# Two class look-ups, one on each half of the TensorE rows, in a fused conditioning kernel

## The reference, cut to what matters

```
h = _ln(x, pw_g[pathway_ids], pw_b[pathway_ids])
h = _ln(h, cp_g[compartment_ids], cp_b[compartment_ids])
t = _ln(x, tm_g[time_steps], tm_b[time_steps])
s = _ln(x, ms_g[scale_type], ms_b[scale_type])
m, n, r = x + _mlp_ln(...)            # one vector per batch entry each
cat = concat([w0*h, w1*t, w2*m, w3*n, w4*r, w5*s])
out = x + _ln(silu(cat @ W1 + b1) @ W2 + b2, g, b)
```

## Time and profile before

| what | value |
|---|---|
| time, median of 3 runs | 1038.83 us (1038.68 to 1039.85) |
| the profiled execution's own time | 1037.92 us |
| its span in the profile | 1036.0 us |
| granted TensorE clock, mean | 0.982 |

### The profile page before, as it was taken

One profiled execution on the slowest core, in us unless ns is written; L12 is line 12 of the kernel. 1 busy time (PEld: TensorE's weight loads), 2 busy tenths in 40 slices (PEclk: granted clock), 3 DMA queues, 4 the chain that ended last, 5 costly groups with the idle time before them and its releaser, 6 DMA issues.

```text
span 1036.0 us, 13671 instructions
## 1 busy us (share of the span) xinstructions
PE 973.5 (94%) x4404; PEld 800.4 (77%) x4404; DVE 805.5 (78%) x1103; ACT 267.7 (26%) x330; POOL 527.3 (51%) x625
## 2 busy tenths in 40 slices
PE   0968799999999999999999999999999999999994
PEld 0755578888888888888888888888888888888883
DVE  4953686969788787978878787978879697978844
ACT  2431222313122222223132231323132232312220
POOL 5650353737555463746555473745555374654311
PEclk9969989999999999999999999999999999999998
DMA  8466254553446354453545455443635445343121
GB/s 303 143 202 226 72 178 97 157 148 118 147 100 203 81 181 123 152 145 84 187 91 188 98 172 141 137 130 91 209 75 181 119 154 150 105 159 91 51 61 40
DMA packets 52786, 142.19 MB, mean 137 GB/s; under 512 B 10233, under 2 KB 10505, under 8 KB 48673
## 3 DMA queue, kind: packets, MB, share of 16 engines
q0 software_dynamic: 23168, 66.60, 26.0%
q1 hardware_dynamic: 29600, 75.37, 20.8%
HBM read 125.04 MB, written 16.91 MB: 137 GB/s over the span
## 4 chain that ended last, share of the span: by engine, by line
PE 90%; DVE 4%; DMA 2%; POOL 1%; issue 1%; SPq 0%; DVEq 0%; ACT 0%; POOLq 0%; ACTq 0%
PE hid_ps L1143 22%; PE hid_ps L1145 22%; PE hid_ps L1144 22%; PE o_ps L1225 5%; PE o_ps L1223 5%; PE o_ps L1224 5%; PE made_ps L1123 3%; PE made_ps L1136 3%; PE hid_ps L1148 1%; DMA y_sb<-ms_g 1%; PE o_ps L1084 0%; DMA r_sb<-res_W 0%; DVE yst L777 0%; DVE xc L716 0%; POOL xrs L387 0%
## 5 line engine op out<-in xcount | busy, mean ns | idle before, releaser
L1143 PE MATMUL hid_ps<-cat_hi,w_hi 128*128 128x512 f32 x1024 | 404.6, 395 | 27.2 <-POOL w_lo L463 25.2
L1144 PE MATMUL hid_ps<-cat_lo,w_hi 128*128 128x512 f32 x1024 | 400.8, 391 | 0.0
L1145 PE MATMUL hid_ps<-cat_hi,w_lo 128*128 128x512 f32 x1024 | 400.7, 391 | 0.0
L1143 PEld LDWEIGHTS hid_ps<-cat_hi,w_hi 128*128 128x128 f32 x1024 | 193.7, 189 | 68.6 <-issue 26.0
L1145 PEld LDWEIGHTS hid_ps<-cat_hi,w_lo 128*128 128x128 f32 x1024 | 193.6, 189 | 40.9
L1144 PEld LDWEIGHTS hid_ps<-cat_lo,w_hi 128*128 128x128 f32 x1024 | 193.7, 189 | 39.2
L445 POOL DMA_INDIRECT pw_rows<-cp,class_now x64 | 131.0, 2046 | 59.7 <-DVE y_sb L768 48.9
L581 ACT ACTIVATE cat_hi<-v_ring 128x1024 fp32r<-128x1024 f32 x64 | 68.0, 1062 | 307.1 <-DVE v_ring L750 307.1
L438 POOL DMA_INDIRECT pw_rows<-pw,path_now x64 | 101.6, 1587 | 61.2 <-DVE y_sb L786 41.0
L385 POOL TENSOR_TENSOR fve<-fmv,eps_col 128x1 f32<-128x1 f32 x64 | 40.1, 626 | 155.9 <-DVE fmv L805 155.9
L459 POOL DMA_DIRECT2D r_sb<-x x60 | 57.8, 964 | 111.1 <-DVE r_sb L834 100.4
(11 more groups left out here) (124 smaller groups left out, 1204.5 us busy)
## 6 DMA issues: line engine op xcount, KB each, us to landing
x_sb<-x SPq DMA_DIRECT2D x16, 1024.0 KB, 6.1
xc<-xT SPq DMA_DIRECT2D x16, 1024.0 KB, 5.0
out<-r_sb SPq DMA_DIRECT2D x64, 256.0 KB, 2.0
r_sb<-x POOLq DMA_DIRECT2D x60, 256.0 KB, 4.8
stats_bc<-token_stats SPq DMA_DIRECT2D x30, 256.0 KB, 5.0
ids_sb<-ids SPq DMA_DIRECT2D x16, 256.0 KB, 7.2
keep<-int_W SPq DMA_DIRECT2D x12, 256.0 KB, 6.5
r_sb<-int_W SPq DMA_DIRECT2D x12, 256.0 KB, 7.4
```

The source lines that it names most:

```text
L1143: pe.matmul(acc, w1_hi[:, k, cols], hi, start=start, stop=False)
L1144: pe.matmul(acc, w1_hi[:, k, cols], lo, start=False, stop=False)
L1145: return pe.matmul(acc, w1_lo[:, k, cols], hi, start=False, stop=stop)
```

## The change

The rows of the two tables are placed anew. The classes take partitions 0 to 63 (high part at 0, low part at 16, high part again at 32), the scales 64 to 127 with the same offsets. Each of a fill's two matmuls takes only the 64 partitions of its own table. The partitions that want the high part of the deviation are now 0 to 31 and 64 to 95, those that want the low part 32 to 63 and 96 to 127, so the statistics are read back by four transfers to 32 partitions each in place of two to 64. The low part of the tables no longer begins at a multiple of 32, and it is made by DVE over all partitions with a column of 0 and -1 (`tables()`), no more by POOL; `class_rows` does the same for `class_bias`. The parameter tensor `small` gets two more columns.

```
-HI, LO, AGAIN, SCL = 0, 32, 64, 16
+HI, LO, AGAIN, SCL = 0, 16, 32, 64
...
-                for v in range(2):
-                    sp.dma_start(stats_bc[64 * v:64 * v + 64, :, :, :].rearrange("q p s t -> q (p s t)"),
-                                 stats_dram[v].rearrange("p m -> (p m)").partition_broadcast(64)
-                                 ).then_inc(stats_in[v], 16)
+                for q in range(4):
+                    sp.dma_start(stats_bc[32 * q:32 * q + 32, :, :, :].rearrange("q p s t -> q (p s t)"),
+                                 stats_dram[q % 2].rearrange("p m -> (p m)").partition_broadcast(32)
+                                 ).then_inc(stats_in[q % 2], 16)
...
-            pool.wait_ge(tab_hi_done, 1)
-            pool.tensor_tensor(class_tab[LO:LO + 32, :, :], tab_raw[LO:LO + 32, :, :],
-                               class_tab[LO:LO + 32, :, :].bitcast(f32), ALU.subtract).then_inc(tables_ready, 1)
-            pool.wait_ge(tables_ready, 1)
             x_rstd(0)
             spread_first()
...
+            def tables():
+
+                dve.wait_ge(tab_hi_done, 1)
+                dve.scalar_tensor_tensor(class_tab[:, :, :], class_tab[:, :, :].bitcast(f32), less_low[:, 0:1], tab_raw,
+                                         ALU.mult, ALU.add).then_inc(tables_ready, 1)
+
...
-                dve.tensor_tensor(class_bias[AGAIN:AGAIN + 32, :], o_ps[AGAIN:AGAIN + 32, 1, :],
-                                  class_bias[AGAIN:AGAIN + 32, :].bitcast(f32),
-                                  ALU.subtract).then_inc(class_bias_ready, 1)
+                dve.scalar_tensor_tensor(class_bias[:, :], class_bias[:, :].bitcast(f32), less_again[:, 0:1], o_ps[:, 1, :],
+                                         ALU.mult, ALU.add).then_inc(class_bias_ready, 1)
...
                 x_low(0, 0)
                 x_low(0, 1)
+                tables()
                 sum_blocks(0)
...
                 for i in range(2):
-                    ins = pe.matmul(made_ps[:, i, :], class_tab[:, i, j * P:(j + 1) * P], scaled[:, :],
+
+                    rows = slice(SCL * i, SCL * i + 64)
+                    ins = pe.matmul(made_ps[:, i, :], class_tab[rows, i, j * P:(j + 1) * P], scaled[rows, :],
                                     start=True, stop=True)
```

More of the change, by code:

```diff
@@ L129, in build @@
         b1_cols, ib1_cols = part("b1T"), part("ib1T")
+        less_again, less_low = part("less_again"), part("less_low")
         sT, shifts, fold = part("sT", BATCHES), part("shifts", 5), part("fold")
@@ L413, in spread_first @@
                 pool.wait_ge(first_stats_out, 16)
-                for v in range(2):
-                    pool.dma_start(stats_bc[64 * v:64 * v + 64, :, :, :].rearrange("q p s t -> q (p s t)"),
-                                   stats_dram[v].rearrange("p m -> (p m)").partition_broadcast(64)
+                for q in range(4):
+                    pool.dma_start(stats_bc[32 * q:32 * q + 32, :, :, :].rearrange("q p s t -> q (p s t)"),
+                                   stats_dram[q % 2].rearrange("p m -> (p m)").partition_broadcast(32)
                                    ).then_inc(first_stats_in, 16)
@@ L704, in stats_here @@
                 if isinstance(b, int) and b == 0:
-                    dve.wait_ge(first_stats_in, 32)
+                    dve.wait_ge(first_stats_in, 64)
                 else:
                     for v in range(2):
-                        dve.wait_ge(stats_in[v], 16 * b)
+                        dve.wait_ge(stats_in[v], 32 * b)
             def centre(b):
@@ L1350 @@
     class_of = np.full((P, 1), -1.0, np.float32)
+    less_again, less_low = np.zeros((P, 1), np.float32), np.zeros((P, 1), np.float32)
+    for at in (0, SCL):
+        less_again[at + AGAIN:at + AGAIN + 5] = -1.0
+        less_low[at + LO:at + LO + 5] = -1.0
     for base in (HI, LO, AGAIN):
@@ L1363 @@
         identity=np.eye(P, dtype=np.float32),
-        class_of=class_of,
+        class_of=class_of, less_again=less_again, less_low=less_low,
         b1T=np.concatenate([cols(cond(n + "_b1")) for n in _NETS], axis=1),
@@ L1381 @@
         xT=put("xT", xs.reshape(BATCHES, P, TT, FT, P).transpose(0, 4, 3, 2, 1).reshape(BATCHES, P, FT * TOKENS)),
-        ids=put("ids", np.where((np.arange(P) % 32 < SCL)[:, None], by_column(cls), by_column(scl))),
+        ids=put("ids", np.where((np.arange(P) < SCL)[:, None], by_column(cls), by_column(scl))),
         pid=put("pid", np.stack([pathway.reshape(BATCHES, P, TT), cls.reshape(BATCHES, P, TT)], axis=2)
```

## The result

| | before | after |
|---|---|---|
| median | 1038.78 us (4 runs, 1038.68 to 1039.85) | 1047.63 us (4 runs, 1046.29 to 1051.13) |
| ratio, 95% interval | | 1.0085 [1.0065, 1.0105] |
| profiled execution, span | 1037.92, 1036.0 | 1051.13, 1049.2 |

The change makes the kernel 8.85 us slower; 10.7 were forecast. The profiled execution of after is the longest of its four, 3.5 us above their median, so times are taken from the medians and the traces are used for where they go.

What follows compares the result with a forecast made beforehand. PE's stream was taken to bound the steady part; 11.0 for the fills, -1.1 for the start and +0.8 for reading back made +10.7 us on 1038.83, so 1049.5 us, with 1037 to 1057 for 8 in 10.

Steps and rivals of the forecast that it cites:

- What bounds: Steady part: PE's stream sets the time, with no PE idle time in a 58.93 us chunk, which becomes 59.7.
- Side by side, and the price of the shape: Each steady fill: 0.23 us saved by running side by side, 0.42 paid for two shape changes, 0.19 more.
- The step with the least behind it: Fill matmuls: 96 partitions read as full size, 64 as a small shape like 32, without a row for 64.
- The rival with no change of shape: Fills: halves run side by side with loads hidden, -13.3 us on the fills, 1025.2 us in all; chance 0.15.
- The rival with one change hidden: Fills: only one of the two shape changes holds the load, -1.2 us, 1037.3 us in all; chance 0.08.
- The rival in which the halves do not overlap: Fills: matmuls don't overlap, +24.4 us, 1062.9; chance 0.04, within 0.09 shared with loads one after the other.
- 58 fills: Of 64 fills, all but chunk 0's four and chunk 1's first two pay 0.19 us each, +11.0 us.
- The start: Program start: without POOL's subtraction, `sum_low` begins at about 22.8 instead of 23.85, -1.1 us, between -2.6 and +0.6.
- the step that copied their duration: Start, POOL: statistics begin at about 9.95, 3.7 us sooner, and the small write is issued at 16.05.
- The landing I took at the middle: Start: the small write takes 4.25 us, between 2.68 and 5.81, since it comes by POOL's queue; lands at 20.3.
- Reading back: Chunk 1: two more statistics reads on SP's queue delay the last transfer, +0.8 us, between 0 and 1.1.
- The sum: Whole kernel: 11.0 - 1.1 + 0.8 = +10.7 us, forecast median 1049.5 us; chance 0.68.

Runs made afterwards that it cites:

- rows_96: The changed kernel with both fill matmuls on partitions 0 to 95, low parts of the scales left out of the picks: 1039.22 us, ratio 1.0005 to the kernel before.
- same_half: The changed kernel with both matmuls of a fill on partitions 0 to 63, scale part of the result left out: 1061.26 us, ratio 1.0217 to the kernel before.
- two_bias: The changed kernel, tables re-placed: in chunks 2 to 15 the first fill's two matmuls run beside two bias matmuls on 32-partition blocks, three statistics reads: 1034.41 us.
- full_rows: The changed kernel with each fill matmul on all 128 partitions again, everything else as changed: 1035.75 us, ratio 0.9972 to the kernel before.
- bias_beside: The changed kernel with the second fill's two matmuls and four bias matmuls on 32-partition blocks, other fills full size, two-level statistics reads: 1091.95 us, ratio 1.0531.

## Why the prediction was right

**What bounds.** Right. Each of the 13 steady chunks grew by 0.80, from 58.93 to 59.73, with no idle time of PE that another engine answers for.

**Side by side, and the price of the shape.** Right, in each of its three parts. Entry 0.32 forecast, 0.32 measured; second matmul 0.01 forecast, none visible; exit with an open load of 0.11, then 0.34 to the successor, as forecast. That makes 0.18 up to the second matmul behind the fill, where 0.19 was forecast. A fourth part was in no term: the next four starts come 0.02 later in all (0.228 to 0.236 apart, not 0.227). So the whole price is 0.20 a fill, and that it is so close to 0.19 is in part luck. The step with the least behind it, that 64 partitions act like 32 and not like 96, was borne out by after, rows_96 and same_half. The rival with no change of shape (1025.2) needed the fill's load to start with the matmul ahead; it starts 0.32 later. The rival with one change hidden fails on the same rows: both loads are held. The rival in which the halves do not overlap is what same_half looks like, 60.62 a chunk and 1061.26 us, near its 1062.9.

The Trainium skill, page TensorEngine Tiling (Array Packing), section Tiling Modes, Key Properties, says that a change of the tiling mode drains the engine while a change of tile does not. By that rule the trace agrees in both halves: both loads at a border are held, and the two halves of the rows run together. It gives no price; here it is 0.41 us for the way in and out. The Trainium skill, page TensorE: Matmul & The Clock Gate, Part 3, Measured speedup vs the span model, counts about one matmul for several on separate row blocks. That holds for what is inside the group (four in two_bias take 0.50, as long as two) and leaves out the border, which decides the sign here.

**58 fills.** 58 x 0.20 = 11.6, against 11.9 from the medians. The traces of after and full_rows differ by 14.3: 11.1 from the first fill of chunk 2 on (56 fills), and 3.2 before it, of which 2.35 are there at the very first fill, where the start of the profile after was slow. So the steady part is shown to a tenth, and the agreement of the rest is not.

**The start.** In the profile after it came out the other way: PE's first matmul was 0.34 later than before, not 1.1 sooner. In full_rows, which has the same start, the direction was right, and two sizes were not. POOL's statistics began at 9.95 there, as forecast. But the step that copied their duration was mis-sized: from their start to the small write I counted 6.1 us, as before, and it is 4.7, since most of the operations now come ahead of DVE's passes and are not slowed by them. The landing I took at the middle, 4.25, because the write has its own queue; it is 5.4, near the upper end, so that queue did not spare it the load. The two nearly cancel, by luck: `sum_low` at 22.45 where 22.8 was forecast, PE's first matmul at 23.82 where 24 was (25.22 before), so -1.4 for -1.1.

**Reading back.** Wrong in sign. +0.8 was forecast for chunk 1, where the last of four reads should have come later. From the first issue to the start of `scaled` there were 6.76 us before (110.37 to 117.13), 6.46 after and 6.04 in full_rows, and DVE's wait shrank from 2.88 to 2.62 and 1.93: the smaller transfers land sooner by more than the further issues cost. In full_rows the second fill of chunk 1 stands at 129.05 and stood at 130.62, 1.6 sooner, and the forecast for that point was 0.3. By the first fill of chunk 2 (183.78 and 184.96) 1.2 of it are left.

**The sum.** 11.9 - 3.2 = 8.7 against 11.0 - 0.3 = 10.7. The error of 2 us is made of -2.9 in the start and the reading back and +0.9 in the shape, which partly cancel. Of the 3.2 the two traces show 1.1 to 1.6; those are single executions, and that of full_rows is the longest of its nine. Where the other 1.6 to 2.1 us between the medians come from stays open.

## What to carry to other kernels

Before work is put on a part of the PE array, count the borders: going from full-size matmuls to 64 or 32 partitions and back costs 0.41 us here, and each matmul that runs beside another saves 0.23. A pair loses 0.2, four together gain a little, and it only reaches the end if the engine that feeds the group keeps its lead. A short chain of small operations with a DMA round trip at the start of a kernel is worth looking at first: moving independent work into the wait, with one pass of DVE put earlier, gave 4.5 us, more than any rearranging of the array. And a rearrangement that makes PE wait can cost twice, by the wait and by the lower clock behind it, as in bias_beside.

## What the runs showed of the hardware that was not expected

- POOL's small operations of L402 to L408, on 4 columns, took 0.19 to 0.20 us when they started before DVE's passes of 1024 columns with two inputs, and 1.05 to 1.19 when they started beside them, until the pass beside them ended. A shift of 0.53 us at 10 us grew to 1.84 at the write. This can make a part of the spread of after's runs, 1046.29 to 1051.13; one trace of each kernel does not settle it.
- Matmuls on 96 partitions hold no load, and yet a chunk with four fills of them takes 59.15 us, not 58.93. The matmuls behind 64 and 32 partitions also stand a little further apart for some starts (0.02 us in all behind a fill of after). The runs don't show why.
- Reads whose source alternates between two rows of DRAM (an outer level of two, an inner one of 16) let DVE start 12.2 us after the last issue, where plain reads of the same bytes land in 4.4 us. Which property of that form makes them late was not tried.
- A write of 8 KB by POOL's queue landed in 5.3 to 5.4 us while the loads filled the DMA engines (share 1.05), and in 2.7 before, at a share of 0.68.
- In bias_beside, with waits of PE of 2.4 us a chunk on the mean (31.4 in 13), the clock was at its lower level eight times between 200 and 1000 us. And at 94 to 110 us both kernels with four matmuls side by side had 10.2 us at that level that the full-size ones had not.
